# Macaron block on one core: new Y ahead of the first softmax's maxima, new Y and W in halves over both banks

## The reference

```python
x = x + 0.5 * ffn(layernorm(x))
x = x + attention(layernorm(x))
x = x + 0.5 * ffn(layernorm(x))

# attention, per batch and head; q_l and k_l are means over 8 tokens (64 landmarks)
s1 = softmax(q @ k_l.T)      # 512 x 64
s2 = softmax(q_l @ k_l.T)    # 64 x 64
s3 = softmax(q_l @ k.T)      # 64 x 512
z = s2.T / (max column sum * max row sum)
for _ in range(6):
    xz = s2 @ z
    z = 0.25 * z @ (13 I - xz @ (15 I - xz @ (7 I - xz)))
out = (s1 @ (z @ (s3 @ v))) @ Wo + bo
```

## Time and profile before

| | us |
|---|---|
| median of 3 runs (lowest, highest) | 1156.12 (1154.26, 1157.37) |
| profiled execution | 1155.66 |
| its span, first to last instruction | 1153.8 |
| TensorE busy | 1088.2 (94%) |
| VectorE busy | 758.1 (66%) |
| ScalarE busy | 584.3 (51%) |
| GpSimd busy | 565.5 (49%) |
| attention stage | about 388 to 780 |

### The profile page before, as it was taken

The page is one execution under the profiler, slowest core; times in us unless marked ns, Lnnn a source line. Parts: engine busy times, 40 slices in busy tenths (PEclk is TensorE's granted clock), DMA queues, the critical chain, the costliest instruction groups (busy, mean ns, idle before and its releaser), DMA issues.

```text
span 1153.8 us, 30074 instructions
## 1 busy us (share of the span) xinstructions
PE 1088.2 (94%) x11278; PEld 878.9 (76%) x11279; DVE 758.1 (66%) x1401; ACT 584.3 (51%) x961; POOL 565.5 (49%) x774
## 2 busy tenths in 40 slices
PE   8999999999999678899999998779999999999997
PEld 6788888888888557677667677558888888888886
DVE  6736746676767557778878867655346566767674
ACT  4334336666665445465465564344443256566663
POOL 5720734667675624345435442336301726666664
PEclk9999999999999887999999999889999999999999
DMA  7272144222211210000000000004241242212220
GB/s 255 74 306 96 37 147 143 61 73 68 68 60 38 92 56 2 3 3 3 3 3 3 3 3 3 20 21 182 92 183 37 73 161 69 64 62 61 73 64 14
DMA packets 39472, 80.25 MB, mean 70 GB/s; under 512 B 6452, under 2 KB 31159, under 8 KB 38336
## 3 DMA queue, kind: packets, MB, share of 16 engines
q1 hardware_dynamic: 27568, 52.94, 12.8%
q0 software_dynamic: 11232, 25.20, 7.1%
q10 hardware_dynamic: 560, 0.52, 0.1%
HBM read 57.13 MB, written 27.00 MB: 73 GB/s over the span
## 4 chain that ended last, share of the span: by engine, by line
PE 83%; DVE 9%; ACT 3%; issue 2%; POOL 2%; DMA 1%; ACTq 0%; DVEq 0%; POOLq 0%
PE PS L1735 19%; PE PS L1649 12%; PE PS L1749 12%; PE PS L1665 7%; PE PS L1823 3%; DVE A_NM L805 3%; PE PS L1742 3%; PE PS L1933 3%; PE PS L1946 2%; PE PS L1833 2%; PE PS L1580 2%; PE PS L1683 2%; PE PS L1961 1%; PE PS L1893 1%; PE PS L1867 1%
## 5 line engine op out<-in xcount | busy, mean ns | idle before, releaser
L1735 PE MATMUL PS<-WHL,XGH 128*128 128x512 f32 x624 | 217.4, 429 | 2.1 <-DVE WHL L679 2.1
L1749 PE MATMUL PS<-WD,XNT 128*128 x624 | 149.7, 383 | 1.5 <-ACT XNT L1129 1.5
L1490 POOL TENSOR_TENSOR A_W<-A_XC,CB 128x256 f32<-128x256 f32 x96 | 69.8, 748 | 153.0 <-DVE A_XC L896 131.4
L700 DVE SCALAR_TENSOR_TENSOR XNT<-PS,SCORES,XNT 128x512 f32<-128x512 f32 x78 | 58.6, 751 | 120.5 <-PE PS L1735 109.9
L1398 POOL DMA_INDIRECT X<-xs_dram,WHO x78 | 103.2, 1323 | 57.6 <-issue 23.1
L1124 ACT ACTIVATE XNT<-PS,SCORES 128x512 f32<-128x512 f32 x78 | 53.8, 689 | 145.7 <-PE PS L1735 143.7
L1735 PEld LDWEIGHTS PS<-WHL,XGH 128*128 128x128 f32 x624 | 111.4, 189 | 20.4 <-DVE WHL L679 2.6
L1749 PEld LDWEIGHTS PS<-WD,XNT 128*128 128x128 f32 x624 | 112.6, 190 | 16.0 <-issue 2.2
L1735 PE MATMUL PS<-WHL,XGL 128*128 128x512 f32 x312 | 123.2, 395 | 0.0
L1392 POOL TENSOR_SCALAR XNT<-WD 128x128 f32<-128x128 f32 x64 | 52.5, 840 | 128.7 <-DVE WD L573 128.7
L1665 PE MATMUL PS<-SDH,HHL 128*128 128x256 f32 x512 | 103.9, 287 | 1.7 <-DVE X L613 1.3
(11 more groups left out here) (273 smaller groups left out, 2527.0 us busy)
## 6 DMA issues: line engine op xcount, KB each, us to landing
xs_dram<-WG SPq DMA_DIRECT2D x16, 512.0 KB, 3.0
WU<-in_r_up SPq DMA_DIRECT2D x2, 4096.0 KB, 15.1
shared_dram<-X SPq DMA_DIRECT2D x16, 512.0 KB, 2.9
WG<-in_r_gate SPq DMA_DIRECT2D x2, 4096.0 KB, 17.1
WD<-in_r_down SPq DMA_DIRECT2D x4, 2048.0 KB
X<-in_x SPq DMA_DIRECT2D x7, 512.0 KB, 9.1
X<-mid_dram SPq DMA_DIRECT2D x7, 512.0 KB, 3.9
X<-xs_dram,WHO POOLq DMA_INDIRECT x78
```

What stands on the lines that cost most here:

```text
L700: dve.scalar_tensor_tensor(B["RH"][:, u * F:(u + 1) * F], banks[3 + u][:], score(t), B["RS"][:, u * F:(u + 1) * F], ALU.mult, ALU.mult).th ...
L1490: pool.tensor_tensor(B["W"][:].rearrange("p (a m) -> p a m", m=M)[:, part, :], B["XC"][b % 2][:].rearrange("p (a w) -> p a w", w=XW)[:, pa ...
L1735: ins = pe.matmul(banks[bank][:], tok, w[:, k * F:(k + 1) * F], start=(k == 0 and i == 0), stop=(k == KD - 1 and i == 2))
L1749: ins = pe.matmul(banks[7][:, 0:D], B["HT"][:, u * F + f * P:u * F + (f + 1) * P], B["WD"][:, bass.ds(ex * (KF * D) + f * D, D)], start=(f ...
```

## The change

The work of the kernel stays the same; its order and the grain of some steps change.

1. W and X are made in steps by pairs of heads. One instruction of `chain_w` and `chain_x` now covers two of the four pairs in both banks, where it covered all four of one bank. `chain_first` waits for the first half of W only, and for the second half in the middle of the product.
2. In the tail of a period, the column sums and maxima of `nxt` and the product of its first Y come before the first softmax's maxima; these wait for Y. The second half of the first softmax's maxima (`s1_max(nxt, 1)`) comes behind the last `chain_second`.
3. `turn_nm1`, the copy to `NM1T`, the copy to `QBDR` and the landmarks of K move into the head of the next period, where also `denominators` moves ahead of `heads(old, 1)`. The second half of the third softmax's maxima (`s3_max(nxt, 1)`) moves behind the output projection and the transposes.
4. In the first expert tile of each FFN, the clearing of `RY` on VectorE moves behind a low part of the tokens and of the weights.

The core of the diff:

```diff
+    def half_pairs(ap, n, w):
+        return ap.rearrange("p (c a w) -> p c a w", c=KD, w=w)[:, :, n * PC // 2:(n + 1) * PC // 2, :]
...
-                if first:
-                    dve.memset(B["RY"][:], 0.0).then_inc(s["ry_clear"], 1)
                 if ahead >= 2:
                     low_tile(t + 2, (u + 2) % UNR)
                 if ahead >= 1:
                     low_weights("WU", ex[u + 1], 2 * t + 3, (2 * u) % 3)
+                if first:
+                    dve.memset(B["RY"][:], 0.0).then_inc(s["ry_clear"], 1)
...
-                low = M if it == PINV_ITERS - 1 else 0
                 dve.wait_ge(att["c2_ready"], count("c2_ready", b, it + 1))
-                for c in (1, 0):
-                    x = chain(b)[:, c * PC:(c + 1) * PC, low:]
-                    dve.scalar_tensor_tensor(x, x, Y_KEPT, pairs(banks[c][:, 0:CW], XW)[:, :, low:], ALU.mult, ALU.add).then_inc(att["x"], 1)
+                for n in range(2):
+                    if it == PINV_ITERS - 1:
+                        x = chain(b)[:, n * PC:(n + 1) * PC, M:]
+                        product = pairs(banks[n][:, 0:CW], XW)[:, :, M:]
+                    else:
+                        part = slice(n * CW // 2, (n + 1) * CW // 2)
+                        x = B["XC"][b % 2][:].rearrange("p (c z) -> p c z", c=KD)[:, :, part]
+                        product = PS[:, 0:KD * 512].rearrange("p (c z) -> p c z", c=KD)[:, :, part]
+                    dve.scalar_tensor_tensor(x, x, Y_KEPT, product, ALU.mult, ALU.add).then_inc(att["x"], 1)
...
                 if exists(nxt):
-                    s3_max(nxt, 0)
+                    landmarks(nxt, 1, 0)
+                    landmarks(nxt, 1, 1)
                 if exists(old):
                     denominators(old)
+                if exists(nxt):
+                    s3_max(nxt, 0, (0,))
                 chain_x(b, 0)
                 if exists(nxt):
-                    s3_max(nxt, 1)
+                    s3_max(nxt, 0, (1,))
+                    s3_max(nxt, 1, (0, 1))
...
-                for n, c in enumerate((1, 0)):
-                    if it == 0:
-                        if n == 0:
-                            wait_alone(att["y0"], count("y0", b, 2))
-                    else:
+                if it == 0:
+                    wait_alone(att["y0"], count("y0", b, 2))
+                    wait_alone(att["c1_ready"], count("c1_ready", b - 1, PINV_ITERS))
+                for n in range(2):
+                    if it:
                         wait_alone(att["x"], count("x", b, 2 * (it - 1) + n + 1))
...
-                pe.wait_ge(att["w"], count("w", b, 2 * it + 2))
+                pe.wait_ge(att["w"], count("w", b, 2 * it + 1))
                 past_waits()
                 for c, p, i in IN_QUADRANTS:
                     q = c * PC + p
+                    if (c, p, i) == (0, PC // 2, 0):
+                        pe.wait_ge(att["w"], count("w", b, 2 * it + 2))
...
                 chain_first(b, 0)
+                if exists(b):
+                    pe.wait_ge(att["s1m"], count("s1m", b, 4))
+                    pe.wait_ge(att["qk"], count("qk", nxt, 4))
+                    turn_nm1(b)
```

More of the change, by code:

```diff
@@ L793, in key_rows, with s3_max @@
                 block_diagonal(B["KBD"][b % 2], B["KL"], "kbd")
-            def s3_max(b, c):
+            def s3_max(b, c, part):
                 dve.wait_ge(att["s3max_ready"], count("s3max_ready", b, c + 1))
-                for k in range(2):
+                for k in part:
                     dve.tensor_reduce(B["NM3"][:].rearrange("p (a s) -> p a s", a=PC)[:, 2 * k:2 * k + 2, c], grid(2 * k, 2).rearrange("p (a l) -> p a l", l=GW), AX_X, ALU.max,
@@ L1005, in attention_vector @@
                     query_block(far)
-                    landmarks(far, 1, 0)
-                    landmarks(far, 1, 1)
             first_low(1)
@@ L1251, in attention_scalar @@
                 chain_b(b, 0)
+                if exists(nxt):
+                    act.wait_ge(att["qbd"], count("qbd", nxt, 1))
+                    act.copy(B["QBDR"][:], B["QBD"][:]).then_inc(att["bdr"], 1)
+                if exists(b):
+                    act.wait_ge(att["nm1_ready"], count("nm1_ready", b, 1))
+                    act.copy(B["NM1T"][:], banks[7][:]).then_inc(att["nm1"], 1)
                 if exists(old):
@@ L1310, in attention_scalar @@
                     product_kept(nxt)
-                    act.wait_ge(att["nm1_ready"], count("nm1_ready", nxt, 1))
-                    act.copy(B["NM1T"][:], banks[7][:]).then_inc(att["nm1"], 1)
-                if exists(far):
-                    act.wait_ge(att["qbd"], count("qbd", far, 1))
-                    act.copy(B["QBDR"][:], B["QBD"][:]).then_inc(att["bdr"], 1)
             first_high(1)
@@ L1991, in attention_tensor @@
                 chain_first(b, 0)
+                if exists(b):
+                    pe.wait_ge(att["s1m"], count("s1m", b, 4))
+                    pe.wait_ge(att["qk"], count("qk", nxt, 4))
+                    turn_nm1(b)
+                if exists(old):
+                    if b == 1:
+                        pe.wait_ge(s_picks, 5)
+                    pe.wait_ge(att["num"], count("num", old, 1))
+                    denominators(old)
                 if exists(nxt):
@@ L1994, in attention_tensor @@
                     pe.wait_ge(att["qkr"], count("qkr", nxt, 3))
-                    pe.wait_ge(att["y0"], count("y0", b, 2))
+                    pe.wait_ge(att["s1m"], count("s1m", b, 4))
                     s3_max(nxt, 0)
@@ L2000, in attention_tensor @@
                     heads(old, 1)
-                    if b == 1:
-                        pe.wait_ge(s_picks, 5)
-                    pe.wait_ge(att["num"], count("num", old, 1))
-                    denominators(old)
                 if nxt == 0:
@@ L2033, in attention_tensor @@
                         turn(far, 1)
+                if exists(nxt) and nxt > 0:
+                    pe.wait_ge(att["qkr"], count("qkr", nxt, 4))
+                    pe.wait_ge(att["s3m"], count("s3m", nxt, 2))
+                    s3_max(nxt, 1)
                 chain_first(b, 1)
@@ L2127, in attention_tensor @@
                     spread_denominators(old)
+                if exists(far):
+                    if far > 0:
+                        pe.wait_ge(att["qk"], count("qk", far, 2))
+                    pe.wait_ge(att["cs"], count("cs", nxt, 1))
+                    project_qk(far, 2)
                 chain_second(b, 4)
                 if exists(nxt):
+                    pe.wait_ge(att["ot"], count("ot", old, 2))
                     pe.wait_ge(att["e3"], count("e3", nxt, 4))
+                    pe.wait_ge(att["e1"], count("e1", b, 4))
+                    start_y(nxt)
                     pe.wait_ge(att["rs"], count("rs", nxt, 1))
                     pv(nxt, 1)
-                    pe.wait_ge(att["ot"], count("ot", old, 2))
-                    pe.wait_ge(att["e1"], count("e1", b, 4))
+                    pe.wait_ge(att["y0"], count("y0", nxt, 2))
                     pe.wait_ge(att["qkr"], count("qkr", nxt, 2))
@@ L2138, in attention_tensor @@
                     s1_max(nxt, 0)
-                    pe.wait_ge(att["qk"], count("qk", far, 3))
-                    pe.wait_ge(att["tts"], count("tts", nxt, 1))
-                    column_sums(nxt)
                 if b == NG - 1:
@@ L2149, in attention_tensor @@
                     first_turn(1)
+                if exists(far):
+                    pe.wait_ge(att["tts"], count("tts", nxt, 2))
+                    project_qk(far, 3)
+                if exists(nxt):
+                    pe.wait_ge(att["qk"], count("qk", far, 3))
+                    pe.wait_ge(att["tts"], count("tts", nxt, 2))
+                    pe.wait_ge(att["cs"], count("cs", nxt, 1))
+                    turn_sums(nxt)
+                chain_second(b, 5)
                 if exists(nxt):
@@ L2166, in attention_tensor @@
                     start_t(nxt)
-                    pe.wait_ge(att["qk"], count("qk", far, 4))
-                    turn_nm1(nxt)
             last = NG - 1
```

42 lines of the change are left out of this document (15 added, 27 removed).

## The result

| | before | changed |
|---|---|---|
| median, us (lowest, highest) | 1155.19 (1154.11, 1157.37), 4 runs | 1163.21 (1161.49, 1163.92), 4 runs |
| ratio, 95% interval | | 1.0066 (1.0049 to 1.0084) |
| profiled execution, us | 1155.66 | 1161.49 |
| its span, us | 1153.8 | 1159.7 |
| mean granted clock of TensorE | 0.979 | 0.972 |

A forecast was written before the change was run, and what follows sets the result against it. TensorE was taken to set the end, with VectorE's unbroken string delaying it at each period's head. The terms 7.8 - 3.5 - 2.0 - 0.5 - 1.2 = +0.6 gave 1156.3, as median 1157 us; range 1146 to 1169.

The forecast's parts named there:

- the three chances: Whole kernel against before, about 0.3% counting as no change: slower 0.38, faster 0.32, the same 0.30.
- Both new waits: TensorE, inner periods: about 0.9 us before the third projection and about 1.8 us before the landmark scores.
- The tail and the head: Inner period: the tail gains VectorE nothing; the head's VectorE string is 12.47 us, S(1) starting 25.16 after first(4).
- The sum of +1.3 a period: Inner period, first(4) to second(1): 26.20 us against 24.89, bounds 0.5 and 2.0.
- the wait of 0.9: Tail of a period: TensorE idles 0.9 us before the third projection, queued behind VectorE's column maxima.
- The six periods together: Six inner periods at +1.3 us each: +7.8 us, bounds 3 to 12.
- The last full period and the last batch: Batch 6's first(4) to batch 7's second(0): -3.5 us; four first products in the last batch waiting for half of W: -2.0.
- the case which the prediction had priced at -1.5: Last full period: if the clock falls there again, only -1.5 us in place of -3.5.
- The start of batch 0: Batch 0: early W starts first(0) at 432.8, but VectorE's string holds second(1) to about 444.2: -0.5 us.
- The clearing of RY: First expert tile of each FFN: clearing moved behind the low part of the weights, -1.2 us, bounds -1.4 and 0.
- its own sign: Landmark scores: clock granted at 0.5 behind their wait in more than one period decides for the clock's fall.
- the rival with a chance of 0.20: Inner periods: the clock falls in the jam, in four of six periods +11 us, 1168 us; chance 0.20.

The follow-up runs named there:

- e3: Changed kernel with Q's landmarks and block diagonal and K's first landmarks moved out of the head into VectorE's gaps: 1167.94 us.
- e9: Changed kernel with the reordered head of e7, but the landmarks left where the changed kernel has them: 1157.17 us.
- e7: e3 with the third softmax's maxima ahead of denominators and reciprocal, their second product directly behind second(0), ScalarE's copies in matching order: 1150.79 us.
- e13: e5 with a useless second projection of the heads in TensorE's wait before the landmark scores, from batch 2 on: 1157.52 us.
- e8: e7 with the column sums and column maxima moved back as in e5: 1143.21 us.
- e2: Kernel before with only the clearing of RY moved behind the low part of the weights: 1154.35 us.
- e12: Changed kernel with a useless second projection of the heads in TensorE's wait before the landmark scores, from batch 2 on: 1157.91 us.
- e10: e3 with a useless second projection of the heads in TensorE's wait before the landmark scores, from batch 2 on: 1156.83 us.
- e5: Changed kernel with the column sums behind second(4) and their maxima one place back on VectorE: 1166.62 us.
- e11: e8 with useless 128x256 matmuls in TensorE's waits of the last two batches: 1139.48 us.
- e4: Changed kernel with K's landmarks in the head made twice on VectorE, the second time into an unused buffer: 1179.55 us.

## Why the prediction was right, and where not

**The mechanism.** 1163.2 lies in the range, 6 above the value; slower by over 0.3% had the largest of the three chances, 0.38, while the value itself stood for no change. Both new waits stand where they were foreseen: 0.78 (forecast 0.9) and 1.83 (forecast 1.8). The periods are 44.4 (forecast 44.9), and batch 7 starts and runs 1.6 shorter (forecast about 5). So the way the kernel gets slower in a period was right, and the sum was not: its terms missed by several us each, and the range was wide enough to hold them.

**The tail and the head.** The sum of +1.3 a period was too high: 0.85 in clear periods. The tail was 0.34 shorter than its steps (second maxima's product 11.64 behind first(4), not 11.98), and the head 0.09. The reason given for the head, that VectorE's queue holds it, is half of it. Priced one for one by that reason, e3 should have won 1 us or more a period, and it won none. TensorE's order, denominators ahead of the maxima's product, is a second string of the same length (e3, e9, e7). And the wait of 0.9, taken as part of the price, can't be won by itself: with it away, in e13 and e8, one of 0.7 for new Y stood in its place, and no period was shorter.

**The six periods together.** From second(1) of batch 0 to first(4) of batch 6 it takes 279.87 before and 286.93 after, +7.1 where +7.8 was forecast. That this is so near is luck: six times 0.85 is 5.1, the two falls of the clock, which the sum left out, add about 3.3, and the idle time of the period from 563.50, which the kernel before had and the prediction didn't mention, takes about 1.7 off; 0.3 is left over.

**The last full period and the last batch.** This is the term that was most off: -3.5 and -2.0 forecast, -0.7 and -0.9 measured. In the profiled execution batch 7's second(0) came 20.92 behind first(4) of batch 6 (753.08 less 732.16), not 18.2, as the clock fell there again, from 743.5. That is the case which the prediction had priced at -1.5. In the last batch the waits for W fell from 3.2 to 1.8, but the products still wait for S, 2.8 before and 2.2 after (two of 1.1 in both kernels). So first(4) comes 1.5 sooner behind second(0), and second(4) only 0.8: GpSimd's half was early, the chain behind the product gave about half of it back.

**The start of batch 0.** -0.5 forecast. second(1) stands at 445.23, 0.55 later than in the earlier trace rows, although the attention's first transposes came 0.9 earlier: +1.4. All of it arises ahead of the first landmark scores, which stand 1.5 later behind those transposes than before; from the scores to second(1) it takes 36.7, and took 36.8. In between the clock was low for 3.4 us in the changed kernel and not before (changed, then before):

```profile
402.10:405.50 3.40, 3.40 (x21) 3.17 (x19) 1.34 (x2) 0.59 (x1) 2.83 (x7) 0.51 0.30 85
```

```profile
402.00:405.40 3.40, 3.36 (x28) 2.90 (x27) 2.26 (x2) 1.34 (x3) 2.71 (x9) 1.00 0.44 154
```

Whether the change brings this fall isn't shown. Behind the scores the clock was low for 19 us up to second(1) in both kernels. There first(0) did come 2.2 sooner, at 433.41 (forecast 2.8), but second(1) only 0.1 sooner by this count, not 0.5.

**The clearing of RY.** -1.2 forecast, and -1.15 in the medians of e2, with the reservation made there. In the changed kernel's profiled execution 0.9 of it is seen in the first FFN and 0.1 in the second.

**The clock.** The forecast took full clock as the likelier, and by its own sign (0.5 at the landmark scores in more than one period) the rival with a chance of 0.20 came true: two periods. Its price, four periods and 1168, did not. e12 shows what filling the idle wait is worth in the median: with it filled the changed kernel is at 1157.9. Of its 8.0 us over before 5.3 go with the filler, and 2.7 are left for all the rest (2.4 against the kernel before as timed beside e12; the forecast was +0.6). So what the value lacked is for the most part the clock, which the sum had put at nothing. In the two profiled executions the 5.3 can't be put to places one by one: they differ by 3.6; 1.3 of it lies in the inner periods and 2.7 ahead of batch 0, where no filler stands, and the rest cancels but for 0.4 the other way. That idle time is the cause of the falls in the covered places is shown by three pairs (e3 and e10, e5 and e13, and in the last batches e8 and e11), in which 11 falls went when the wait was filled.

The Trainium skill (TensorE: Matmul & The Clock Gate, Why this matters for your kernels), which warns of idle gaps longer than any in the inner periods, would have had no fall there. The runs decide against reading it that way: a single wait of 1.83, ahead of the scores at 534.85, was followed by the fall at 535.3, and filling such waits took such falls away.

## What to carry to other kernels

When an engine's order and another engine's queue hold the same point, taking one away shows nothing: test them together before you call either hidden. A wait on TensorE has two prices, the idle time and the half clock that can follow; look at the granted clock behind every cluster of waits. Here waits of 0.7 to 0.8 and 1.8 in each period brought anything from two to six falls in six periods, so compare periods without a fall before you judge a change of order. Where such a wait can't be removed, useless matmuls in it can pay, as 12 of them did here, if their bank is free and they end about when the data arrives.

## What the runs showed of the hardware

- A fall of the clock cost an inner period 1.0 to 2.3 us (those of e3 and e4 against their clear ones, those of e5 against the clear ones of e13), and in the period into the last batch filling the wait was worth up to 5.5 (49.76 in e3, 44.28 in e10).
- Stretches alike in busy time came out differently: in e8 TensorE was busy for 2.19 of 3.40 us ahead of the fall at 725.0, and in the changed kernel for 2.18 where none came. What was computed in them differs, and what decides wasn't measured.
- The mean granted clock of one kernel differed from execution to execution: 0.963 to 0.972 in the six runs of e5, whose times are 1160.5 to 1168.3.
